# GpSimd adds a layer's output bias to the residual rows one body later: a two-layer cross-attention kernel on one Trainium2 core

## The reference, cut to what matters

```python
# stage 0: per batch, a linear attention over 1x1 convolutions, batch norm, + x      (result: x, 2048 rows x 512)
for i in (1, 2):                                   # two cross-attention layers, 16 heads of 128
    res = x
    h = layer_norm(x, ln_scale_i, ln_offset_i)
    q, k, v = h @ wq + bq, ctx @ wk + bk, ctx @ wv + bv         # k, v get one more key: bias_k, bias_v
    x = res + softmax(q @ k.T / sqrt(128)) @ v @ wo + bo_i      # bo_i: the layer's output bias, one row of 512
h = gelu(layer_norm(x) @ w_fc1 + b_fc1) @ w_fc2 + b_fc2         # b_fc2: the third output bias
out = x + h
```

## Time and profile before

| | |
|---|---|
| median of 3 runs | 2394.24 us |
| the profiled execution | 2392.99 us |
| its span, first to last instruction | 2391.1 us |
| PE busy | 2348.5 us (98%) |
| DVE busy | 1330.6 us (56%) |
| ACT busy | 1142.5 us (48%) |
| POOL busy | 464.1 us (19%) |
| share of the chain that ended last | PE 90%, ACT 4%, DVE 4%, POOL 0% |

### The profile page before, as it was taken

How to read it: one execution, slowest core, us unless ns; L and a number is a source line. 1 busy time by engine, 2 the same in 40 slices (tenths; PEclk the granted TensorE clock), 3 DMA queues, 4 the chain that set the end, 5 groups by cost and what they waited for, 6 DMA issues and landing times.

```text
span 2391.1 us, 32423 instructions
## 1 busy us (share of the span) xinstructions
PE 2348.5 (98%) x12304; PEld 1995.5 (83%) x12304; DVE 1330.6 (56%) x2328; ACT 1142.5 (48%) x2717; POOL 464.1 (19%) x280
## 2 busy tenths in 40 slices
PE   8999999999999899999999989999999999999999
PEld 7777788888888688888888878888888887788887
DVE  4444453454454666666666676666666666644433
ACT  3222222222223566666666677666666667322222
POOL 2111121121233500111001244111001115611110
PEclk9999999999999999999999999999999999999999
DMA  7454565666666424333333423333333331100001
GB/s 273 168 191 167 182 220 212 239 220 217 234 221 221 168 100 144 125 120 137 132 126 124 135 96 124 129 117 137 127 134 124 129 129 45 45 18 27 27 1 70
DMA packets 142168, 331.83 MB, mean 139 GB/s; under 512 B 8896, under 2 KB 74944, under 8 KB 125632
## 3 DMA queue, kind: packets, MB, share of 16 engines
q1 hardware_dynamic: 141296, 329.68, 39.4%
q10 hardware_dynamic: 720, 0.10, 0.0%
HBM read 190.81 MB, written 138.94 MB: 138 GB/s over the span
## 4 chain that ended last, share of the span: by engine, by line
PE 90%; ACT 4%; DVE 4%; issue 1%; DMA 0%; POOL 0%; ACTq 0%; DVEq 0%
PE U L576 23%; PE U L578 23%; PE U L577 23%; PE T L670 4%; PE O L576 2%; PE S L578 2%; PE O L578 2%; PE O L577 2%; PE S L576 2%; PE S L577 2%; DVE hT L999 1%; ACT aff L809 1%; ACT probs L850 1%; ACT probs L842 1%; DVE gT L1009 1%
## 5 line engine op out<-in xcount | busy, mean ns | idle before, releaser
L1018 DVE TENSOR_TENSOR x<-x,U 128x512 f32<-128x512 f32 x384 | 260.8, 682 | 79.9 <-PE U L578 77.5
L842 ACT ACTIVATE probs<-S,nm 128x257 f32<-128x257 f32 x512 | 238.0, 476 | 40.4 <-DVE nm L1026 40.3
L1026 DVE TENSOR_REDUCE nm<-S 128x2 f32<-128x514 f32 x256 | 177.3, 692 | 123.8 <-PE S L578 119.9
L860 ACT ACTIVATE PT<-T 128x512 fp32r<-128x512 f32 x256 | 152.6, 596 | 172.9 <-PE T L670 172.5
L850 ACT ACTIVATE probs<-probs,rs 128x256 f32<-128x256 f32 x512 | 230.1, 499 | 1.3 <-DVE rs L1030 1.1
L798 ACT ACTIVATE stage<-tmp 128x512 fp32r<-128x512 f32 x128 | 80.9, 632 | 308.8 <-DVE tmp L991 308.8
L576 PE MATMUL U<-wos,oT 128*128 128x512 f32 x512 | 213.5, 417 | 0.4 <-DVE oT L1041 0.4
L791 ACT ACTIVATE stage<-U,hc 128x512 fp32r<-128x512 f32 x128 | 88.3, 690 | 259.4 <-PE U L578 259.4
L983 DVE SCALAR_TENSOR_TENSOR stage<-U,hc,stage 128x512 fp32r<-128x512 f32 x128 | 96.0, 750 | 206.7 <-ACT stage L791 206.5
L576 PE MATMUL U<-wvs,cT 128*128 128x512 f32 x512 | 206.1, 403 | 0.0
L458 POOL CAST wos<-raw 128x1024 fp32r<-128x1024 f32 x20 | 20.8, 1040 | 952.1 <-PE U L578 952.1
(11 more groups left out here) (166 smaller groups left out, 5818.2 us busy)
## 6 DMA issues: line engine op xcount, KB each, us to landing
kd<-stage SPq DMA_DIRECT2D x128, 516.0 KB, 3.1
kb<-kd SPq DMA_DIRECT2D x64, 1032.0 KB, 4.8
vd<-stage SPq DMA_DIRECT2D x128, 512.0 KB, 3.2
vb<-vd SPq DMA_DIRECT2D x64, 1024.0 KB, 5.1
raw<-wa SPq DMA_DIRECT2D x24, 512.0 KB, 5.9
raw<-wb SPq DMA_DIRECT2D x24, 512.0 KB, 5.9
raw<-wk SPq DMA_DIRECT2D x16, 512.0 KB, 6.0
raw<-wv SPq DMA_DIRECT2D x16, 512.0 KB, 5.7
```

Of the source, the lines that this page charges most:

```text
L842: ins = act.activation(probs[:, r, qt, 0:257], S[:, qt, 0:257], ACT.Exp, bias=nm[:, r, qt:qt + 1], scale=-1.0, accum_out=sums[:, r, qt:qt ...
L860: act.activation(PT[:, J % 2, 0, :], T[:], ACT.Copy).then_inc(pt_hi, 1)
L1018: dve.tensor_tensor(x[:, tile, :], x[:, tile, :], bank(what, s, t), ALU.add).then_inc(free, 1)
L1026: dve.tensor_reduce(nm[:, J % 2, :], S[:, :, 0:257], AX.X, ALU.min).then_inc(least, 1)
```

## The change

`add_bias` no longer stands behind the norm's rows. The four additions of a chunk now wait until DVE has added the chunk's last unit of the layer's first body (`w(s,3)` of that step, semaphore `free`) and are issued in the layer's second body, or second perceptron body. DVE's wait for `ln_bias` moves from the first body's outputs to the second body's. The load of the next `brow` moves one body later on SP. The number of instructions and what they compute stay as they were, but for the order in which bias and first outputs are added to x.

```diff
@@ SP, bodies of attention
                     if c == 1:
                         load_o(E + 1)
-                        if E in (1, BODIES + 1):
+                        if E in (2, BODIES + 2):
                             bias_row(1 + E // BODIES)
@@ POOL
             def add_bias(n, c):
 
                 pool.wait_ge(brow_in, n * 16 + 16)
-                pool.wait_ge(ln_z, n * TILES + 4 * c + 4)
+                first = ("w", n * BODIES * CHUNKS + c, 3) if n < LAYERS else ("W", c, 3)
+                pool.wait_ge(free, UNIT[first] + 1)
                 for t in range(4 * c, 4 * c + 4):
                     pool.tensor_tensor(x[:, t, :], x[:, t, :], brow[:], ALU.add).then_inc(ln_bias, 1)
@@
             normalise(0, 1)
-            add_bias(0, 0)
             normalise(0, 2)
             normalise(0, 3)
-            for c in range(1, CHUNKS):
-                add_bias(0, c)
             queries(1)
             for E in range(HBODIES):
                 last = E % BODIES == BODIES - 1
@@
                 if last:
-                    normalise(n, 0)
-                    normalise(n, 1)
-                    add_bias(n, 0)
-                    normalise(n, 2)
+                    for c in range(3):
+                        normalise(n, c)
+                if E % BODIES == 0:
+                    for c in range(3):
+                        add_bias(E // BODIES, c)
                 outputs(E + 1)
+                if E % BODIES == 0:
+                    add_bias(E // BODIES, 3)
                 if last:
                     if n < LAYERS:
                         normalise(n, 3)
                     else:
                         deviation(n, 3)
-                    for c in range(1, CHUNKS):
-                        add_bias(n, c)
             for E in range(HBODIES, HBODIES + MBODIES - 1):
                 queries(E + 1)
+                if E == HBODIES:
+                    for c in range(3):
+                        add_bias(LAYERS, c)
                 outputs(E + 1)
+                if E == HBODIES:
+                    add_bias(LAYERS, 3)
@@ DVE, output
-                if t == 0 and what == "w" and s % (BODIES * CHUNKS) < CHUNKS:
+                if t == 0 and what == "w" and s % (BODIES * CHUNKS) // CHUNKS == 1:
                     dve.wait_ge(ln_bias, s // (BODIES * CHUNKS) * TILES + 4 * (s % CHUNKS) + 4)
-                if t == 0 and what == "W" and s < CHUNKS:
-                    dve.wait_ge(ln_bias, LAYERS * TILES + 4 * s + 4)
+                if t == 0 and what == "W" and s // CHUNKS == 1:
+                    dve.wait_ge(ln_bias, LAYERS * TILES + 4 * (s % CHUNKS) + 4)
```

## The result

| | before | changed |
|---|---|---|
| median of the runs | 2394.31 us (6 runs, 2391.11 to 2402.33) | 2374.09 us (6 runs, 2372.96 to 2374.65) |
| the profiled execution | 2392.99 us, span 2391.1 | 2373.61 us, span 2371.8 |

The ratio is 0.9909, with a 95% interval of 0.9891 to 0.9927: the changed kernel is faster by 0.9%. Two of the six runs before took over 2402 us and enter this ratio; the medians alone give 0.9916. Between the two profiled executions 19.4 us are gone, where the prediction had 15.7. The median of 2374.09 us lies 4.5 us under the 2378.6 us forecast, at the lower edge of the range (2374). By the ratio the change is larger than the range allows: 0.9909 of the 2394.24 us that the prediction started from is 2372.5 us.

A forecast was written before the change was run, and what follows sets the result against it. PE, busy 98% of the span, was taken to bound the kernel, with the gain in its stops. The terms -11.8 - 1.9 - 2.0 = -15.7 us gave 2377.3 profiled, plus 1.25 for the median: 2378.6 us, range 2374 to 2386.

The forecast's parts named there:

- The mechanism: POOL's additions and DVE rows that both read two SBUF operands exclude each other, so PE waits and its clock falls.
- -11.8: Norm 0: -12.4 us for the piece of twelve removed, 0.55 added for one delayed `hT` row in step 1.
- -1.9: Norm 1: -2.5 us for the piece of twelve removed, 0.55 added for one delayed `hT` row in step 33.
- -2.0: Perceptron: `z` ends 3.4 us sooner, `gT` rows about 2 us sooner; delays at new pieces taken off; bounds +0.3 and -4.0.
- the front: Before norm 0's lock-out, a `stage` row took 4.26 us beside four additions; PE was said to lose nothing: 0.
- in all of them or in none: Three runs lay within 1.5 us, so norm 0's 12 us were taken to be in every run, as in the profile.
- the pieces of four: Rival, chance 0.2: the lock-out moves along and lasts to the end of each piece; -11.6 us, 2382.6 us.
- the small terms: Rival, chance 0.06: norm 0's 11.15 us has another cause, only 1.9 + 2.0 = 3.9 us go; 2390.3 us.
- plain steps cost nothing: Against the rival, chance 0.03, that additions also hold DVE's PSUM rows in plain steps: 22 us lost, 2400 us.
- The 11.15 us row: DVE's `hT` row in norm 0, 0.69 us if free, said to end when POOL's piece of twelve additions has ended.
- At 0.74 that is 0.55: Chunk 0's new piece delays one `hT` row by 0.75 us, priced at 0.74 us per us: 0.55 us each layer.
- The bound of -4.0: Perceptron: the largest gain allowed, if all PE stops but the weights' go, with the filling of the pipeline.

The follow-up runs named there:

- one_operand: The kernel before, each addition replaced by `(x - 0) * 1` on POOL, which reads one tile in place of two: 2373.49 us, 0.9876 of before.
- late_joined: The changed kernel with a layer's additions of chunks 0 to 2 in one piece of twelve in plain steps: 2374.5 us, ratio 0.9903.
- late_1: The kernel before with only norm 1's additions moved to the second body: median 2389.73 us, ratio 0.9977.
- late_2: The kernel before with only the additions of the perceptron's bias moved: median 2387.56 us, ratio 0.997.
- late_0: The kernel before with only norm 0's additions moved to the second body: median 2390.21 us, ratio 0.9975; 5 of 12 runs at 2379.57 to 2380.92.
- before_drain: The kernel before, with POOL waiting for its own last addition before it issues the next: 2380.32 us, 0.9927 of before.

## Where the prediction was right, and where it failed

**What failed.** The mechanism held, and the sum -15.7 was too small. Its terms were -11.8, -1.9, -2.0 and nothing for the front; measured were -12.45, -2.65, -3.33 and -0.86. The perceptron is mis-sized most. The front, set to nothing, is what carries the total of 19.29 us past the largest gain that the prediction allowed, 18.9 us: the other three give 18.43. Of the 4.5 us by which the median missed, 3.7 are these terms; the other 0.8 are the 1.25 us added for the median above the profiled execution, where the changed kernel has 0.48. And the step "in all of them or in none" left no room for a second loss of about 12 us that only some executions of before have; they are what puts the ratio beyond the range.

**Mechanism and direction: right.** The stretch behind `w(0,3)` went from 70.79 to 58.33 us at clock 1.00, no DVE row beside an addition is above 3 us (the longest `hT` or `gT` row is 1.65), `hT` has one delayed row in steps 1 and 33 (1.45 and 1.47 us in a forecast of 1.4 to 2.7), and the additions come in twelve pieces. one_operand shows that additions with two tile operands on POOL's side are needed, late_joined that plain steps don't mind. The rivals fall: the pieces of four didn't lock DVE out in any of the 12 runs of the changed kernel (spread 2.2 us), more than the small terms came, and plain steps cost nothing.

**Two rows were read too simply.** The 11.15 us row was said to end with POOL's piece. The piece ends at 834.50 us, the row at 824.88 + 11.15 = 836.03. Between them lies this row of POOL's timeline of before:

```profile
834.43 1.05 POOL L458 CAST wqs_b<-raw 128x1024 fp32r<-128x1024 f32 x1
```

If the row needs its usual 0.69 us, it was by these rows let in at about 835.3, with the cast nearly done. The cast reads one tile, so "two tiles on both sides" doesn't describe the whole lock-out; why this cast held the row and one_operand's instructions didn't stays open. And the 2.20 us row of rows 7 starts at 1460.78, when norm 1's twelve additions had ended at 1458.50: it met the split behind them, 1.51 us of waiting, more than one addition. Only two of the three waits there are waits for additions.

**Norm 0 and norm 1: the term added was mis-sized.** "At 0.74 that is 0.55": the delayed `hT` row was put at 0.55 us in each layer, on top of an undisturbed 58.4 us. The measured stretches are 58.33 and 58.37 us with that row in them, and taking it away gives 0.12 and 0.11. The 0.74 us per us of delay came from three delayed rows one after the other; a single one of 0.76 us cost 0.12. A price per us that was read from several delays isn't the price of one. The estimate of 58.4 itself, from the step lengths of rows 6, was right to 0.2 us. With 0.12 for 0.55 the terms are -12.3 and -2.4, against -12.45 and -2.65 measured.

**Front: a term set to nothing.** "PE had work and lost nothing there" was said of the 4.26 us row. It cost 0.82 us by late_1, where the row is 1.74 us, and the change gave back 0.86. The wait of PE comes 22 us behind the row (1.33 us in place of 0.50), and I had looked for one right behind it; the way to see it was to compare the length from one `z` to the next with what it is in an undisturbed run.

**The perceptron: -2.0, measured -3.33.** Three pieces of the term were off, each to the safe side; no run prices them apart. `z` takes 1.91 us for four when free, where 2.46 was taken from another operation of the same size, which is simply slower. The two `gT` rows behind it were expected to be held to boundaries; they took 0.78 and 1.07 us. The piece starts at 2033.10, when `z` has ended (2032.35), and DVE waits for ACT's high part ahead of each. And the rows that meet an addition in the next steps take 1.65 us at most, where one behind a split was to take 2.0 to 2.6 us and cost PE 0.6 in all. PE's waits in the changed kernel have only 0.3 us for `gT` (the view of waits; us in all, times, longest):

```profile
PE U L580 <- DVE gT L1013: 0.3, 1, 0.3
PE U L617 <- DVE hT L1003: 0.2, 1, 0.2
```

The bound of -4.0 held.

**"So the 12 us of norm 0 are in all of them or in none": half right, and on too few runs.** late_1 and late_2 show the norm 0 row at 11.16 us again, with late_0's and the changed kernel's parts 12 us below, and none of the 20 runs of late_1 and late_2 is under 2387 us, so norm 0 did belong to the median. But three runs that agree don't exclude a second meeting that goes either way: in 29 runs of before, 8 lie about 12 us higher. The 12 runs of the changed kernel have no such group (2372.96 to 2375.12), so the change also takes away a spread that the prediction didn't know of: set against 11 runs of before of which 5 were upper ones it gives 0.9902.

**The rule that was weighed.** The sum by the Trainium skill's "SBUF — State Buffer", "Who interferes with whom", one whole instruction of waiting at most, was -5.8; the row of 11.15 us was measured, and the change gave 19.3. before_drain shows where the rule does hold: with 0.17 us between additions no `hT` row beside them in norms 0 and 1 is above 1.29 us, 0.6 more than its own 0.69. The rule describes one meeting of two instructions. For a queue that issues the next one without a gap, the run of instructions can act as one.

## What to carry to other kernels

Look for a row on one engine that is many times its usual length and ends when a run of back-to-back instructions on the other ends: here VectorE and GpSimd each reading two tiles from SBUF. The remedies tried here, in order of worth, are to move one side to steps where the other reads PSUM (19.3 us), and to let the engine wait for its own last instruction between two of them (12.6 us between the profiled executions, two added lines). And where such a meeting decides 12 us by chance, three runs don't tell how a kernel behaves; compare parts of the span between marks that all kernels share.

## What the runs showed of the hardware that I had not expected

- The length of a lock-out isn't fixed by the program. The same `stage` row beside the same four additions took 4.26 us in one execution and 1.74 us in those of three kernels that keep the additions there; norm 0's row was 11.15 to 11.16 us in three profiles of three, each 5.3 us into the piece. The phase doesn't decide it alone: the `stage` row began 1.4 us into its piece both ways. What does stays open.
- 0.17 us of POOL waiting for itself ends it in norms 0 and 1. "GPSIMD Engine Reference", "2.1 Instruction dispatch", of the Trainium skill, by which the cores start the next instruction each for itself, would explain why a run without gaps holds the ports; that the gap cures it agrees with this, and no row shows the cores apart.
- DVE's `z`, which reads one tile and two columns, waits as well: 1.91 us for four alone, 5.83 beside two-operand additions, 3.13 beside one-operand instructions of POOL, while `hT` with its two tiles is hardly held by the latter (0.69 us in norms 0 and 1, 1.08 at most in the perceptron). What holds `z` beside one-operand instructions no run here shows.
- A meeting can be paid by POOL: its one-operand instructions took 2.51 and 2.56 us in place of 2.08 where an `hT` row had begun 0.09 to 0.14 us ahead of them, and the `hT` rows took their 0.69.
- Doing less work can cost time: without the bias additions the perceptron was 1.34 us longer, since splits of weights moved up beside `hT` and `gT` rows.
